# Eight TensorE fillers, squares on ScalarE and weights' low halves on VectorE, in a new order of the first seven units

## Chip, cores and metric

One NeuronCore of one Trainium2 chip. The metric is the device time of one execution, in microseconds (us). TensorE's matmuls, VectorE (DVE), ScalarE (ACT), GpSimd (POOL) and SyncE (SP, which issues the DMAs) run side by side and meet at semaphores.

## What is computed

`x` is 16 x 256 x 256, float32. A layer normalisation, attention with 16 heads of 128 over 4 key/value heads, and a quantised linear layer follow, both added to their input:

```python
x = x + attention(layernorm(x), wq, wk, wv, wo)   # causal, first 4 keys and a window of 32
x = x + ffn(layernorm(x), weight, bias)           # int8-rounded x and weight, 256 -> 256
# attention: q = x wq.T, k = x wk.T, v = x wv.T; softmax(q k.T / sqrt(128), masked) v; then wo.T
```

## The kernel before

Work is cut into 64 **units**: unit u is batch `b = u // 4` and key/value group `g = u % 4`, with its four query heads. Every matmul of the attention runs in float16 with each operand split into a high half (rounded) and a low half (what rounding left), and three products for the pairs high-high, high-low, low-high (`PAIRS`).

The steps of a unit are functions on each engine's queue. On TensorE: `q_fill(u, f)` (L436, half f of the queries, 12 matmuls), `scores(u)` (L466, 27), `p_transpose(u)` (L510, 9), `pv(u, j)` (L539, L540) and `out_proj(u)` (L557, 24); per batch `x_transpose` (L392), `k_fill` (L404) and `v_fill` (L415). What they leave in PSUM is taken out in two steps: ScalarE makes the high half (`q_high` L829, `k_high` L816, `v_high` L824, `o_high` L875), then VectorE subtracts it from PSUM for the low half (`q_low` L1044, `k_low` L1034, `v_low` L1039, `o_low` L1071). The softmax goes VectorE `s_mask` (L1052), `s_peak` (L1057), GpSimd `s_shift` (L1439), ScalarE `exps` (L836), VectorE `probs` (L1062 to L1066), GpSimd `p_norm` (L1450), ScalarE `p_high` (L865), GpSimd `p_low` (L1456), TensorE `p_transpose`, ScalarE `pt_evac` (L845). The normalisation is `ln_stats` (L1018), `ln_rstd` on GpSimd, `ln_norm` (L1028, writes `xn`), `ln_split` on ScalarE and `ln_low` (L1408) on GpSimd.

**Weights.** Before its first use each weight tile (k, v, q0 to q3, o0 to o3; 128 x 1024 numbers each) gets one power of two as its scale. ScalarE sums the squares (`weight_squares`, L799, an activation with an accumulator, read out by a second instruction); TensorE adds that over the partitions and spreads it (`scale_sums`, L367); VectorE makes the scale (`scale`, L1162 to L1167); ScalarE writes the high half (`weight_high`, L805) and VectorE the low half (`weight_low`, L1182: one `scalar_tensor_tensor` with the weight and its high half as inputs, both in SBUF). Four things are different. The output weights' squares are made by GpSimd (`squares`, L1418) and summed by TensorE over columns (`column_sums`, L379, 8 matmuls of one column each a tile), a `column_copy` (L1186) on VectorE putting the sum where `scale_sums("o")` reads it. The low halves of v, o2 and o3 are made by GpSimd in two instructions each (`weight_scaled` L1427, `weight_low` L1433). The scale of k stands first, and the first thing on TensorE is 13 products of `small_ones` with itself (L641) whose result nobody reads.

**Order.** Every engine runs its queue in order. For the units up to the scores of unit 6 the order of calls is written out by hand for each engine; from t = 7 on a loop `for t in range(FIRST, NU - 3)` gives each engine the same turn: scores(t), pv(t-2), both halves of q_fill(t+1), one k or v fill of the next batch, p_transpose(t-1), out_proj(t-2) and what VectorE, ScalarE and GpSimd owe to them. An order for the last three units follows, again by hand. Before the loop TensorE does out_proj(4) last; `scores(7)` opens the loop. A second line of waits: `scores(u)` needs both q_low(u), and from unit 2 on also pt_evac(u-2), whose PSUM bank it takes; `q_fill(u, f)` needs q_low(u-1, f); `pv(u, j)` needs o_low(u-1, j).

SyncE issues the loads in one queue: x of batch 0, wk, wq part 0, idh (the identity for transposes), wv, x of batch 1, wq part 1, the mask, wq parts 2 and 3, wo parts 0 to 3, and so on.

## Time and profile before

| | |
|---|---|
| median of 3 runs | 616.41 us (615.7 to 616.91) |
| the profiled execution's own time | 616.56 us |
| its span, first to last instruction | 614.8 us |
| mean granted TensorE clock | 0.988 of 2.4 GHz |
| TensorE busy | 593.4 us, 97% |
| VectorE busy | 544.4 us, 89% |
| ScalarE busy | 394.6 us, 64% |
| GpSimd busy | 337.3 us, 55% |

Busy time is the time in which an instruction of the engine was under way, so an instruction that is held by something outside it counts as busy. In the rows further down a line is an instruction or a group of equal ones: its start, its length, its engine, the line of the code, what it writes and reads, and in square brackets how long its engine was idle before and whose result it waited for. Consecutive instructions of an engine overlap a little, so that lengths add up to somewhat more than the time that passes. A window's line gives the same by stretch.

### The profile page before, as it was taken

The numbers are of one execution on the slowest core, as the hardware profiler recorded it, in microseconds if no ns is written. First come the engines' busy times: TensorE is split into PE (matmuls) and PEld (weight loads), VectorE is DVE, ScalarE is ACT, GpSimd is POOL, SyncE is SP. The second block draws the span as 40 slices with busy tenths as digits, with TensorE's granted clock in tenths as the row PEclk, the third lists the DMA queues.
The fourth block names the chain that finished last, engine by engine and source line by source line (L and its number), as shares of the span: only waits on it lengthen the run. The fifth ranks groups of instructions, "written<-read, shape, count | busy, mean of one in ns | idle before, by whom it ended". The sixth has DMA issues, their size and how long they took to land.

```text
span 614.8 us, 18062 instructions
## 1 busy us (share of the span) xinstructions
PE 593.4 (97%) x7566; PEld 523.8 (85%) x7566; DVE 544.4 (89%) x1072; ACT 394.6 (64%) x617; POOL 337.3 (55%) x320
## 2 busy tenths in 40 slices
PE   7699999999999999999999999999999999999994
PEld 6488878898888989889898988989898898989883
DVE  6999999898998989899898989979898897989886
ACT  6588646656656766665676666667666666765660
POOL 2667753564745556474555647455564645646563
PEclk8899999999999999999999999999999999999997
DMA  8565205060421506042160604316060421505001
GB/s 294 188 139 139 65 24 122 18 156 19 92 67 56 118 18 156 19 99 59 40 135 20 155 18 91 67 39 135 19 138 3 103 54 37 120 19 138 2 19 35
DMA packets 36272, 49.69 MB, mean 81 GB/s; under 512 B 2784, under 2 KB 22240, under 8 KB 36192
## 3 DMA queue, kind: packets, MB, share of 16 engines
q1 hardware_dynamic: 36048, 48.41, 31.9%
q8 instruction: 60, 0.98, 0.7%
q14 instruction: 20, 0.16, 0.1%
q10 hardware_dynamic: 144, 0.13, 0.1%
HBM read 35.42 MB, written 12.58 MB: 78 GB/s over the span
## 4 chain that ended last, share of the span: by engine, by line
PE 83%; DVE 11%; issue 2%; ACT 2%; POOL 2%; POOLq 0%; DVEq 0%; ACTq 0%
PE ps L436 24%; PE ps L557 23%; PE ps L466 8%; PE ps L404 6%; PE ps L415 6%; PE ps L510 4%; PE ps L540 4%; PE ps L539 4%; DVE Qs L1044 1%; DVE xn L1028 1%; PE ps L392 1%; PE ps L641 1%; PE ps L603 1%; DVE WqT L1182 1%; DVE sm L1062 1%
## 5 line engine op out<-in xcount | busy, mean ns | idle before, releaser
L436 PE MATMUL ps<-xT,WqT 128*128 128x256 f16 x1536 | 179.4, 273 | 2.2 <-DVE WqT L1182 1.4
L557 PE MATMUL ps<-WoT,pool 128*128 128x256 f16 x1440 | 167.3, 273 | 1.0 <-DVE pool L1071 1.0
L436 PEld LDWEIGHTS ps<-xT,WqT 128*128 128x128 f16 x1536 | 146.8, 98 | 19.0 <-DVE WqT L1182 1.8
L557 PEld LDWEIGHTS ps<-WoT,pool 128*128 128x128 f16 x1440 | 138.1, 98 | 16.3 <-DVE pool L1071 1.3
L1450 POOL TENSOR_TENSOR small<-E,rr 128x576 f32<-128x576 f32 x64 | 73.9, 1154 | 92.3 <-DVE rr L1066 92.3
L875 ACT ACTIVATE pool<-ps 128x512 f16<-128x512 f32 x128 | 69.9, 594 | 83.9 <-PE ps L540 83.8
L829 ACT ACTIVATE Qs<-ps 128x576 f16<-128x576 f32 x128 | 82.7, 646 | 44.4 <-PE ps L436 44.3
L1456 POOL TENSOR_TENSOR PP<-small,PP 128x576 f16<-128x576 f32 x64 | 82.2, 1284 | 50.3 <-ACT PP L865 50.3
L1439 POOL TENSOR_TENSOR Sm<-Sm,mx 128x576 f32<-128x576 f32 x64 | 74.9, 1170 | 46.2 <-DVE mx L1057 45.0
L1044 DVE TENSOR_TENSOR Qs<-ps,Qs 128x576 f16<-128x576 f32 x128 | 92.9, 727 | 4.5 <-ACT Qs L829 4.5
L1071 DVE SCALAR_TENSOR_TENSOR pool<-ps,pool 128x512 f16<-128x512 f32 x128 | 82.1, 680 | 0.0
L1052 DVE TENSOR_TENSOR Sm<-ps,mask 128x576 f32<-128x576 f32 x64 | 47.6, 744 | 27.7 <-PE ps L466 27.7
L845 ACT ACTIVATE PT<-ps 128x1024 f16<-128x1024 f16 x64 | 66.0, 1031 | 8.6 <-PE ps L510 8.6
L836 ACT ACTIVATE E<-Sm,esc 128x576 f32<-128x576 f32 x64 | 49.6, 774 | 25.8 <-POOL Sm L1439 25.8
L466 PE MATMUL ps<-Kw,Qs 128*128 128x64 f16 x1728 | 61.5, 194 | 4.2 <-DVE Qs L1044 4.0
L466 PEld LDWEIGHTS ps<-Kw,Qs 128*128 128x128 f16 x1728 | 59.1, 98 | 7.6 <-DVE Qs L1044 5.3
L1062 DVE TENSOR_REDUCE sm<-E 128x9 f32<-128x576 f32 x64 | 48.0, 750 | 15.2 <-ACT E L836 15.2
L1057 DVE TENSOR_REDUCE mx<-Sm 128x9 f32<-128x576 f32 x64 | 48.2, 753 | 2.0
L404 PE MATMUL ps<-xT,WkT 128*128 128x256 f16 x384 | 48.4, 277 | 0.3 <-DVE Vn L1039 0.3
L415 PE MATMUL ps<-WvT,xT 128*128 128x512 f16 x192 | 47.4, 383 | 0.4 <-POOL WvT L1433 0.4
L865 ACT ACTIVATE PP<-small 128x576 f16<-128x576 f32 x64 | 43.8, 685 | 2.3 <-POOL small L1450 2.1
L510 PE MATMUL ps<-idh,PP 128*128 128x128 f16 x576 | 42.6, 219 | 0.5 <-POOL PP L1456 0.5
(129 smaller groups left out, 913.7 us busy)
## 6 DMA issues: line engine op xcount, KB each, us to landing
values<-Vn SPq DMA_DIRECT2D x32, 256.0 KB, 2.0
VW<-values SPq DMA_DIRECT2D x16, 480.0 KB
big<-values SPq DMA_DIRECT2D x16, 480.0 KB
X<-in_L_attn_x SPq DMA_DIRECT2D x16, 256.0 KB, 8.4
...
```

Source lines behind the costliest of these rows:

```text
L404: a = pe.matmul(banks[k_bank(b, f)][:, j * 256:j * 256 + 256], WkT[:, k, wl, g * 128:g * 128 + 128], xT[:, b % 2, k, xl, :], start=(n == 1 ...
L415: a = pe.matmul(banks[v_bank(b, t)][:, :], xT[:, b % 2, k, xl, t * 128:t * 128 + 128], WvT[:, k, wl, :], start=(n == 1), stop=(n == 6))
L436: a = pe.matmul(banks[BANK_Q[f]][:, j * 256:j * 256 + 256], WqT[:, k, wl, h * 128:h * 128 + 128], xT[:, b % 2, k, xl, :], start=(n == 1), ...
L466: a = pe.matmul(banks[BANK_S[c]][:, (s - s0) * KEYS:(s - s0 + 1) * KEYS], Qs[:, p, ql, s * 128:s * 128 + 128], Kw[:, b % 2, g, kl, w, :], ...
L557: a = pe.matmul(out_view(b, t), OT[:, p, ol, h, t * 128:t * 128 + 128], WoT[:, 4 * g + h, wl, :], start=first, stop=(end and g == KV - 1), ...
L829: act.activation(dst[0], src, ACT.Copy).then_inc(q_h, 1)
L875: act.activation(OT[:, u % 2, 0, :, cols], src, ACT.Copy, scale=1.0 / P_UP).then_inc(o_h, 1)
L1044: dve.tensor_tensor(dst[1], src, dst[0], ALU.subtract).then_inc(q_l, 1)
L1071: dve.scalar_tensor_tensor(OT[:, u % 2, 1, :, cols], src, 1.0 / P_UP, OT[:, u % 2, 0, :, cols], ALU.mult, ALU.subtract).then_inc(o_l, 1)
L1439: pool.tensor_tensor(Sm[:, p], Sm[:, p], mx[:, p, :].unsqueeze(2).to_broadcast([128, NT, KEYS]), ALU.subtract).then_inc(s_d, 1)
L1450: pool.tensor_tensor(Pn[:, p], E[:, p], rr[:, p, :].unsqueeze(2).to_broadcast([128, NT, KEYS]), ALU.mult).then_inc(p_n, 1)
L1456: pool.tensor_tensor(PP[:, p, :, 1, :], Pn[:, p], PP[:, p, :, 0, :], ALU.subtract).then_inc(p_l, 1)
```

## The change

The four squares of the output weights become `weight_squares` on ScalarE, each with a column of `am` of its own (it grows to 10 columns), and `scale_sums("o")` adds the four columns in PSUM; `column_sums`, `column_copy` and the constant `one` go. The low halves of v, o2 and o3 become `weight_low` on VectorE, and GpSimd does nothing on weights any more (with them go `squares`, `weight_scaled` and GpSimd's `weight_low`). Eight more products of `small_ones` follow the sum of k. idh is loaded ahead of wq part 0. `scale_sums("v")` moves ahead of k_fill(0, 0). Otherwise all calls up to the loop stay, in another order on each of the four queues. The loop and the end are the same. The diff without its first declarations, the constant and the removed GpSimd functions:

```diff

     load_x(0)
     sp.dma_start(w_tile("k"), wk_v).then_inc(ld_k, 16)
+    sp.dma_start(idh[:, :], idh_d).then_inc(ld_idh, 16)
     sp.dma_start(w_tile("q0"), wq_v[0]).then_inc(ld_q[0], 16)
-    sp.dma_start(idh[:, :], idh_d).then_inc(ld_idh, 16)
     sp.dma_start(w_tile("v"), wv_v).then_inc(ld_v, 16)
     load_x(1)
     sp.dma_start(w_tile("q1"), wq_v[1]).then_inc(ld_q[1], 16)
...

         if name == "k":
             pe.wait_ge(cst_ok, 3)
-        elif name != "o":
+        else:

             pe.wait_ge(w_s[SUMS_ORDER[SUMS_ORDER.index(name) - 1]], 1)
-        pe.wait_ge(w_am[name], 1)
-        c = SCALES[name]
-        pe.matmul(all_sums(name), small_ones[:, :], am[:, c:c + 1], start=True, stop=True).then_inc(w_all[name], 1)
-
-    def column_sums(name):
-
-        if name == "o0":
+        if name == "o":

             pe.wait_ge(v_l, 2)
-            pe.wait_ge(cst_ok, 5)
-        pe.wait_ge(w_sq[name], 1)
-        sq = w_squares(name)
-        for h in range(4):
-            for k in range(2):
-                a = pe.matmul(banks[BANK_OUT][:, 0:1], sq[:, h, 128 * k:128 * k + 128], one[:, 0:1],
-                              start=(name == "o0" and h == k == 0), stop=(name == "o3" and h == 3 and k == 1))
-        a.then_inc(w_col, 1)
+        n = KV if name == "o" else 1
+        pe.wait_ge(w_am[name], n)
+        for c in range(SCALES[name], SCALES[name] + n):
+            a = pe.matmul(all_sums(name), small_ones[:, :], am[:, c:c + 1], start=(c == SCALES[name]), stop=(c == SCALES[name] + n - 1))
+        a.then_inc(w_all[name], 1)

     def x_transpose(b):

...
     for _ in range(13):
         pe.matmul(banks[BANK_S[0]][:, 0:128], small_ones[:, :], small_ones[:, :], start=True, stop=True)
     scale_sums("k")
+    for _ in range(8):
+        pe.matmul(banks[BANK_S[0]][:, 0:128], small_ones[:, :], small_ones[:, :], start=True, stop=True)
     pe.wait_ge(ld_idh, 16)
     x_transpose(0)
     scale_sums("q0")
+    scale_sums("v")
     pe.wait_ge(xt_ok, 1)
     k_fill(0, 0)
-    scale_sums("v")
     scale_sums("q1")
     q_fill(0, 0)
     q_fill(0, 1)
+    v_fill(0, 0)
+    v_fill(0, 1)
+    scores(0)
     scale_sums("q2")
-    v_fill(0, 0)
-    scores(0)
-    v_fill(0, 1)
     q_fill(1, 0)
     q_fill(1, 1)
     scale_sums("q3")

     pe.wait_ge(v_l, 1)
     k_fill(0, 1)
-    column_sums("o0")
     scores(1)
-    column_sums("o1")
-    column_sums("o2")
     q_fill(2, 0)
+    q_fill(2, 1)
+    q_fill(3, 0)
     x_transpose(1)
-    q_fill(2, 1)
+    scale_sums("o")
+    q_fill(3, 1)
+    p_transpose(0)

     pe.wait_ge(xt_ok, 2)
     pe.wait_ge(k_l, 2)
     k_fill(1, 0)
-    column_sums("o3")
-    q_fill(3, 0)
-    p_transpose(0)
-    scale_sums("o")
-    q_fill(3, 1)
     scores(2)
+    q_fill(4, 0)
+    pv(0, 0)
+    pv(0, 1)

     pe.wait_ge(k_l, 3)
     v_fill(1, 0)
-    pv(0, 0)
-    pv(0, 1)
-    q_fill(4, 0)

     pe.wait_ge(s_m, 3)
     v_fill(1, 1)
+    q_fill(4, 1)
+    p_transpose(1)

     pe.wait_ge(v_l, 3)
     k_fill(1, 1)
-    p_transpose(1)
-    q_fill(4, 1)
     scores(3)
     q_fill(5, 0)
-    x_transpose(2)
     pv(1, 0)
     pv(1, 1)
+    x_transpose(2)
+    q_fill(5, 1)
     p_transpose(2)
-    q_fill(5, 1)
+    out_proj(0)
     scores(4)
-    out_proj(0)
-    q_fill(6, 0)
+
+    pe.wait_ge(xt_ok, 3)
+    pe.wait_ge(k_l, 4)
+    k_fill(2, 0)
     pv(2, 0)
     pv(2, 1)
+    q_fill(6, 0)
     p_transpose(3)
     q_fill(6, 1)
     scores(5)
-
-    pe.wait_ge(xt_ok, 3)
-    pe.wait_ge(k_l, 4)
-    k_fill(2, 0)
     out_proj(1)
-    q_fill(7, 0)
-    p_transpose(4)
-    pe.wait_ge(k_l, 5)
-    v_fill(2, 0)
-    scores(6)
     pv(3, 0)
     pv(3, 1)
     out_proj(2)
+    p_transpose(4)
+    q_fill(7, 0)
+    scores(6)
     pv(4, 0)
     pv(4, 1)
+    pe.wait_ge(k_l, 5)
+    v_fill(2, 0)
     out_proj(3)
     q_fill(7, 1)
     pe.wait_ge(v_l, 5)
...

         act.wait_ge(w_loaded(name), 16)
         src, hi, _, _ = w_views(name, None)
-        act.activation(hi, src, ACT.Square, accum_out=am[:, SCALES[name]:SCALES[name] + 1]).then_inc(w_am[name], 1)
+
+        n, c = ("o", SCALES["o"] + int(name[1])) if name[0] == "o" else (name, SCALES[name])
+        act.activation(hi, src, ACT.Square, accum_out=am[:, c:c + 1]).then_inc(w_am[n], 1)

     def weight_high(name, js=(0, 1)):
         whole = len(js) == 2
...
     weight_squares("q1")
     weight_high("v")
     k_high(0, 0)
+    q_high(0, 0)
+    weight_high("q1")
+    q_high(0, 1)
     weight_squares("q2")
-    q_high(0, 0)
-    q_high(0, 1)
-    weight_high("q1")
-    weight_high("q2")
     v_high(0, 0)
+    weight_squares("o0")
+    v_high(0, 1)
     weight_squares("q3")
     ln_split(1)
-    v_high(0, 1)
     q_high(1, 0)
+    weight_high("q2")
     q_high(1, 1)
+    weight_high("q3")
+    weight_squares("o1")
     exps(0)
-    k_high(0, 1)
-    weight_high("q3")
+    weight_squares("o2")
     q_high(2, 0)
-    x_evac(1)
+    weight_squares("o3")
     q_high(2, 1)
     p_high(0)
-    k_high(1, 0)
+    k_high(0, 1)
     q_high(3, 0)
+    x_evac(1)
+    weight_high("o0")
     pt_evac(0)
     exps(1)
+    k_high(1, 0)
+    q_high(3, 1)
+    q_high(4, 0)
+    weight_high("o1")
+    p_high(1)
+    o_high(0, 0)
+    ln_split(2)
+    v_high(1, 0)
+    v_high(1, 1)
+    o_high(0, 1)
+    exps(2)
+    pt_evac(1)
+    q_high(4, 1)
+    k_high(1, 1)
+    p_high(2)
     weight_high("o2")
-    weight_high("o0")
-    q_high(3, 1)
-    v_high(1, 0)
-    p_high(1)
-    weight_high("o1")
-    ln_split(2)
-    exps(2)
-    v_high(1, 1)
-    q_high(4, 0)
-    pt_evac(1)
-    o_high(0, 0)
-    o_high(0, 1)
-    p_high(2)
-    q_high(4, 1)
+    x_evac(2)
+    exps(3)
+    pt_evac(2)
+    o_high(1, 0)
     q_high(5, 0)
-    x_evac(2)
-    pt_evac(2)
-    exps(3)
-    k_high(1, 1)
-    o_high(1, 0)
+    o_high(1, 1)
     q_high(5, 1)
-    o_high(1, 1)
     p_high(3)
+    o_high(2, 0)
+    o_high(2, 1)
     q_high(6, 0)
-    o_high(2, 0)
     pt_evac(3)
     exps(4)
-    o_high(2, 1)
     k_high(2, 0)
+    weight_high("o3")
+    q_high(6, 1)
     p_high(4)
-    q_high(6, 1)
-    weight_high("o3")
-    pt_evac(4)
-    v_high(2, 0)
     o_high(3, 0)
     o_high(3, 1)
+    pt_evac(4)
+    o_high(4, 0)
     exps(5)
+    v_high(2, 0)
+    o_high(4, 1)
     q_high(7, 0)
-    o_high(4, 0)
-    exps(6)
     ln_split(3)
     p_high(5)
-    o_high(4, 1)
     q_high(7, 1)
     v_high(2, 1)
+    exps(6)
     pt_evac(5)

     for t in range(FIRST, NU - 3):
...
     weight_low("k", (1,))
     x_evac(0)
     scale("q0")
+    ln_stats(1)
     exp_scale(0)
-    ln_stats(1)
     scale("v")
     weight_low("q0", (0,))
     weight_low("q0", (1,))
     scale("q1")
-    ln_norm(1)
-    exp_scale(1)
+    weight_low("v")
     k_low(0, 0)
-    scale("q2")
     q_low(0, 0)
     q_low(0, 1)
     weight_low("q1")
+    v_low(0, 0)
+    ln_norm(1)
+    scale("q2")
     s_mask(0)
-    v_low(0, 0)
+    v_low(0, 1)
     s_peak(0)
+    scale("q3")
+    q_low(1, 0)
+    q_low(1, 1)
     weight_low("q2")
-    q_low(1, 0)
-    v_low(0, 1)
-    q_low(1, 1)
-    scale("q3")
+    weight_low("q3")
     probs(0)
     s_mask(1)
-    k_low(0, 1)
-    weight_low("q3")
     q_low(2, 0)
     s_peak(1)
     q_low(2, 1)
-    column_copy()
     ln_stats(2)
+    scale("o")
+    k_low(0, 1)
+    exp_scale(1)
+    q_low(3, 0)
+    weight_low("o0")
+    probs(1)
     k_low(1, 0)
-    scale("o")
-    q_low(3, 0)
-    probs(1)
+    exp_scale(2)
+    ln_norm(2)
     s_mask(2)
-    exp_scale(2)
+    q_low(3, 1)
     s_peak(2)
-    ln_norm(2)
+    q_low(4, 0)
     v_low(1, 0)
-    weight_low("o0")
-    q_low(3, 1)
+    v_low(1, 1)
+    o_low(0, 0)
     probs(2)
-    v_low(1, 1)
-    q_low(4, 0)
-    o_low(0, 0)
+    o_low(0, 1)
+    q_low(4, 1)
     s_mask(3)
-    o_low(0, 1)
+    exp_scale(3)
     s_peak(3)
-    q_low(4, 1)
-    exp_scale(3)
+    ln_stats(3)
+    k_low(1, 1)
     weight_low("o1")
-    q_low(5, 0)
     probs(3)
     o_low(1, 0)
+    o_low(1, 1)
     s_mask(4)
-    o_low(1, 1)
+    q_low(5, 0)
+    s_peak(4)
     q_low(5, 1)
-    s_peak(4)
-    ln_stats(3)
-    k_low(1, 1)
     o_low(2, 0)
+    o_low(2, 1)
+    ffn_weight_scale()
+    weight_low("o2")
     probs(4)
-    q_low(6, 0)
     s_mask(5)
     k_low(2, 0)
+    s_peak(5)
+    q_low(6, 0)
     q_low(6, 1)
-    ffn_weight_scale()
-    o_low(2, 1)
-    s_peak(5)
+    o_low(3, 0)
+    o_low(3, 1)
+    weight_low("o3")
+    ln_norm(3)
+    ffn_weight_round()
+    probs(5)
     s_mask(6)
     v_low(2, 0)
-    o_low(3, 0)
-    o_low(3, 1)
     s_peak(6)
-    probs(5)
-    ln_norm(3)
-    o_low(4, 0)
-    probs(6)
     out_scale()
     ffn_residual(0)
+    o_low(4, 0)
     o_low(4, 1)
-    ffn_stats(0)
     q_low(7, 0)
     q_low(7, 1)
-    ffn_weight_round()
+    ffn_stats(0)
+    probs(6)
     v_low(2, 1)

     for t in range(FIRST, NU - 3):
...
     ln_rstd(0)
     ln_low(0)
     ln_rstd(1)
-    weight_scaled("v")
-    weight_low("v")
-    squares("o0")
-    squares("o1")
+    ln_low(1)
     s_shift(0)
-    squares("o2")
-    ln_low(1)
     p_norm(0)
-    squares("o3")
+    s_shift(1)
     p_low(0)
-    s_shift(1)
     ln_rstd(2)
     p_norm(1)
+    p_low(1)
     s_shift(2)
-    p_low(1)
     ln_low(2)
     p_norm(2)
     p_low(2)
     s_shift(3)
-    weight_scaled("o2")
     p_norm(3)
+    ln_rstd(3)
     p_low(3)
     s_shift(4)
-    weight_low("o2")
     p_norm(4)
-    ln_rstd(3)
     p_low(4)
-    weight_scaled("o3")
     s_shift(5)
-    weight_low("o3")
+    p_norm(5)
+    p_low(5)
     s_shift(6)
-    p_norm(5)
     ln_low(3)
-    p_low(5)
+    f_rstd(0)
     p_norm(6)
-    f_rstd(0)

     for t in range(FIRST, NU - 3):
         b, g = divmod(t, KV)
```

## Rows read from the trace of the kernel before

**Rows 1.** Stretches: length, busy PE, PEld, DVE, ACT, POOL, granted clock, DMA, GB/s.

```profile
106.74:586.00 479.26, 478.72 (x6248) 426.57 (x6244) 424.75 (x827) 311.28 (x490) 260.65 (x250) 1.00 0.30 71
...
12.15:50.68 38.53, 31.78 (x350) 25.15 (x348) 35.57 (x65) 28.91 (x44) 26.52 (x19) 0.94 0.59 168
...
51.24:87.60 36.36, 35.01 (x450) 30.15 (x448) 35.32 (x66) 24.50 (x38) 27.59 (x23) 1.00 0.35 81
```

**Rows 2.** Timeline, TensorE, scores of units 3 and 7: start, length, line.

```profile
51.24 0.95 PE L466 MATMUL ps<-Kw,Qs 128*128 128x64 f16 x27
...
87.60 0.95 PE L466 MATMUL ps<-Kw,Qs 128*128 128x64 f16 x27
```

**Rows 3.** The chain of waits, units 7 to 9: start, length, piece.

```profile
98.07 0.06 PE ps L539
...
98.98 2.62 PE ps L436 x24
...
106.74 0.79 PE ps L466 x27
...
112.58 0.50 PE ps L510 x9
```

**Rows 4.** Timeline, VectorE and GpSimd side by side: start, length, engine, line.

```profile
5.99 0.73 DVE L1028 TENSOR_SCALAR xn<-X,mv,rs 128x256 f32<-128x256 f32 x2 [1.18 <-POOL rs L1404]
...
13.95 3.03 DVE L1182 SCALAR_TENSOR_TENSOR WqT<-big,up,WqT 128x512 f16<-128x512 f32 x2
...
17.36 3.65 DVE L1028 TENSOR_SCALAR xn<-X,mv,rs 128x256 f32<-128x256 f32 x2
...
18.93 3.84 POOL L1418 TENSOR_TENSOR WoT<-pool 128x1024 bf16<-128x1024 f32 x2
...
24.02 1.27 DVE L1182 SCALAR_TENSOR_TENSOR WqT<-big,up,WqT 128x1024 f16<-128x1024 f32 x1
...
35.13 2.44 DVE L1182 SCALAR_TENSOR_TENSOR WqT<-big,up,WqT 128x1024 f16<-128x1024 f32 x1
...
69.99 1.89 POOL L1427 TENSOR_TENSOR pool<-pool,up 128x1024 f32<-128x1024 f32 x1 [0.35 <-ACT WoT L805]
...
70.31 1.60 DVE L1197 TENSOR_SCALAR ft<-ft 128x2 f32<-128x2 f32 x1
```

**Rows 5.** Timeline, TensorE at the start, and one stretch with its granted clock.

```profile
1.11 5.74 PE L641 MATMUL ps<-small_ones 128*128 128x128 f32 x26 [1.11 <-DVE small_ones L1229]
...
8.89 0.62 PE L392 MATMUL ps<-idh,xhl 128*128 128x128 f16 x8 [1.92 <-DMA idh<-in_idh]
...
10.52 2.72 PE L404 MATMUL ps<-xT,WkT 128*128 128x256 f16 x12
...
11.00:12.00 1.00, 1.00 (x7) 0.69 (x6) 0.93 (x6) 1.00 (x4) 0.00 (x0) 0.50 1.05 399
```

**Rows 6.** Timeline, VectorE: the scale of q0 and the peak of unit 2.

```profile
10.69 0.16 DVE L1162 TENSOR_SCALAR dn<-ps 128x1 int32<-128x1 int32 x1 [0.26 <-PE ps L367]
...
44.75 0.75 DVE L1057 TENSOR_REDUCE mx<-Sm 128x9 f32<-128x576 f32 x1
```

**Rows 7.** The profile page, part 5: groups of instructions, busy, mean ns, idle before.

```profile
L1439 POOL TENSOR_TENSOR Sm<-Sm,mx 128x576 f32<-128x576 f32 x64 | 74.9, 1170 | 46.2 <-DVE mx L1057 45.0
...
L836 ACT ACTIVATE E<-Sm,esc 128x576 f32<-128x576 f32 x64 | 49.6, 774 | 25.8 <-POOL Sm L1439 25.8
...
L845 ACT ACTIVATE PT<-ps 128x1024 f16<-128x1024 f16 x64 | 66.0, 1031 | 8.6 <-PE ps L510 8.6
```

**Rows 8.** Timeline, one sum of squares on ScalarE with its read-out.

```profile
16.14 1.05 ACT L799 ACTIVATE WqT<-big 128x1024 f16<-128x1024 f32 x1
...
17.09 0.20 ACT L799 ACTIVATION_READ_ACCUMULATOR WqT<-big 128x1 f32 x1
```

**Rows 9.** Waits of ScalarE, 12.15 to 50.7 us: total, times, longest.

```profile
ACT Qs L829 <- PE ps L436: 3.9, 6, 1.0
...
ACT WqT L805 <- DVE up L1167: 2.6, 1, 2.6
```

More of the change, by code:

```diff
@@ L80, in build @@
         diag = sb("diag", [128, 2, 128], F32)
-        am = sb("am", [128, 7], F32)
-        one = sb("one", [128, 2], BF16)
+        am = sb("am", [128, 10], F32)
         up = sb("up", [128, 7], F32)
@@ L176, in build @@
         w_am = {n: sem(f"w_am_{n}") for n in SCALES}
-        w_sq = {n: sem(f"w_sq_{n}") for n in TILES[6:]}
-        w_col = sem("w_col")
         w_all = {n: sem(f"w_all_{n}") for n in SCALES}
@@ L182, in build @@
         w_l = {n: sem(f"w_l_{n}") for n in TILES}
-        w_c = {n: sem(f"w_c_{n}") for n in ("v", "o2", "o3")}
         def w_tile(name):
@@ L205, in w_views @@
             return (w_tile(name)[:, :, n0:n1], wt[:, :, 0, at + n0:at + n1], wt[:, :, 1, at + n0:at + n1], SCALES[name])
-        def w_scaled(name):
-            if name[0] == "o":
-                return w_tile(name)
-            return E[:, :, :, :].rearrange("p u s k -> p (u s k)")[:, 0:1024].rearrange("p (k r) -> p k r", k=2)
         def all_sums(name):
             return banks[BANK_OUT if name == "o" else BANK_O[1]][:, SCALES[name]:SCALES[name] + 1]
-        def w_squares(name):
-            h0 = 4 * int(name[1])
-            return WoT[:, h0:h0 + 4, 1, :].bitcast(BF16)
         x_v = x_d.rearrange("b (t p) d -> b p t d", p=128)
@@ L1230, in _ @@
             dve.memset(ones[:, :], 1.0).then_inc(cst_ok, 1)
-            dve.memset(one[:, :], 1.0).then_inc(cst_ok, 1)
             dve.memset(VW[0][64:128, :, 1, :].bitcast(F32), 0.0).then_inc(z_ok, 1)
@@ L1414, in f_rstd @@
                 pool.tensor_tensor(rs2[:, :, 0], rs2[:, :, 1], cst[:, 2:4], ALU.pow).then_inc(f_rs, 1)
-            def squares(name):
-                pool.wait_ge(w_loaded(name), 16)
-                pool.tensor_tensor(w_squares(name), w_tile(name), w_tile(name), ALU.mult).then_inc(w_sq[name], 1)
-            def weight_scaled(name):
-                src, _, _, c = w_views(name, None)
-                if name == "v":
-                    pool.wait_ge(w_s[name], SCALE_OPS)
-                else:
-                    pool.wait_ge(w_h[name], 2)
-                pool.tensor_tensor(w_scaled(name), src, up[:, c:c + 1].unsqueeze(2).to_broadcast(list(src.shape)), ALU.mult).then_inc(w_c[name], 2)
-            def weight_low(name):
-                _, hi, lo, _ = w_views(name, None)
-                pool.wait_ge(w_h[name], 2)
-                pool.wait_ge(w_c[name], 2)
-                pool.tensor_tensor(lo, w_scaled(name), hi, ALU.subtract).then_inc(w_l[name], 2)
             def s_shift(u):
```

3 lines of the change are left out of this document (removed).

## Prediction

> **What bounds the kernel now.** I read the end first, then walked back. From the second turn of the loop to shortly before the end TensorE is busy for 478.7 of 479.3 us [rows 1]: the loop is bound by TensorE and nothing in it is edited. So the kernel's time is the start of the loop plus a constant. The loop's first instruction is the scores of unit 7, at 87.60 us [rows 2]; the span is 614.8 us and the profiled execution's own time 616.56, so 528.96 us follow that start. The whole question is what happens to 87.60.
>
> I cut the 87.60 us at the scores of unit 3, at 51.24 [rows 2]: stretch A before it, stretch B of 36.36 us behind it. In B the chain of waits gives TensorE's issue cost of each piece [rows 3]: 2.62 us for 24 matmuls of q_fill, hence 1.31 for a half of 12, and the same 1.31 for a k_fill or v_fill and 2.62 for an out_proj, which feed as many columns; 0.79 for a scores; 0.91 for a pv (98.07 to 98.98); 0.50 for a p_transpose of nine, so 0.45 for an x_transpose of eight. B holds 6 q halves, 3 k/v fills, 4 p_transposes, 1 x_transpose, 4 scores, 4 pv and 5 out_proj: 7.9 + 3.9 + 2.0 + 0.45 + 3.2 + 3.6 + 13.1 = 34.1 us. The new order holds the same pieces between the same two points. TensorE's floor for B is 34.1, and the kernel loses only 2.2 us to it. In A it is different: from 12.15 to 50.68 VectorE is busy 35.57 of 38.53 us, TensorE 31.78, ScalarE 28.91, GpSimd 26.52 [rows 1]. VectorE sets the pace, and part of its busy time is no work but waiting inside an instruction, as follows.
>
> **What leaves VectorE's path.** Two xn instructions took 3.65 us from 17.36, and 0.73 at 5.99. The second time GpSimd was at the low half of v and then at squares (3.84 from 18.93). The low half of q3 took 2.44 against 1.27 for q1's of the same size; the two halves of q0's took 3.03 for the same elements [rows 4]. I count 2.9 + 1.2 + 1.5 (3.03 less 1.27 and a second instruction's start, about 0.25) = 5.6 us of stalls in A that lie beside GpSimd's work on weights. That work goes: four squares and the three pairs for v, o2, o3. In B the same shows once, at 70.31: 1.60 us for a two-element instruction under a GpSimd instruction of 1.89 from 69.99 [rows 4], about 1.4 lost.
>
> **What comes onto VectorE.** The low halves of v, o2 and o3, at 1.27 each if undisturbed, v in A and the others in B. The upper bound of one is 2.44 [rows 4]. I take 1.27, because with the weights gone GpSimd runs only softmax steps, and each of these (shift, product, low half of P) is released by VectorE's own reduction or reciprocal just before. The column copy and a memset go, at nothing: one is an element per partition, the other lies in the idle start.
> What the rows show is that VectorE is held only while GpSimd is inside an instruction. The Trainium skill (SBUF — State Buffer, Who interferes with whom) says that a VectorE instruction with two SBUF inputs contends with a GpSimd instruction that reads SBUF, and that whichever issued first holds the other for the whole instruction. A weight's low half has two SBUF inputs, so this speaks against moving three more of them to VectorE; it is the second rival below.
>
> **The first products.** 26 records took 5.74 us [rows 5], 0.22 each, so eight more products are 16 records or 3.5 us, from 6.9 to 10.3. They are no longer covered: x_transpose(0), at 8.89 today [rows 5], starts at 10.3, ends at 10.9, and with its copy on VectorE the scale of q0 starts at 11.6 instead of 10.69 [rows 6]: 0.9 us later. That idh is loaded ahead of q0 on SyncE's queue takes away the wait for it and gains nothing behind these products; q0 is needed by ScalarE later than it lands, so I price its delay at nothing (0.5 at worst). In return the clock: k_fill(0,0) took 2.72 us, twice the 1.31 of an equal fill later, with a granted clock of 0.50, which is 1.2 GHz, after TensorE had stood idle from 6.9 to 8.9 [rows 5]. If the busy engine keeps 2.4 GHz, that fill is 1.3 shorter. It ends ahead of VectorE's and ScalarE's queues either way, so I book zero (0 to 1.0 gained).
>
> **Stretch A, summed.** VectorE ran from the scale of q0 (10.69) to the end of unit 2's peak (44.75 + 0.75 = 45.5) [rows 6]: 34.8 us. Less 5.6 of stalls, plus what now stands ahead of that peak: v's low 1.27, o0's low 1.27, q_low(3,1) 0.65 (an estimate: it passes as many elements as the peak, which took 0.75 with the overlap of its neighbours) and ln_norm(2) 0.73, together 3.9. That gives 33.1 us from 11.6: 44.7. Behind it stand GpSimd's shift 1.17, ScalarE's exponential 0.77 and the copy of PT(1) 1.03 [rows 7], and scores(3) could start at 47.7. Other steps of VectorE (ln_stats, k_low) only swap places within the sum.
> ScalarE has a floor of its own. It worked 28.91 us from 12.15 to 50.68 [rows 1]; its part to the same copy gains four squares at 1.05 + 0.20, counted without overlap [rows 8], 5.0 in all. The high half of o2 leaves and a high half of q0 comes in, which cancels. So 33.9 us from about 12.15: 46.0 if it never waits. It waited 9.6 us before; 2.6 for a scale stuck on VectorE behind the xn stall, 3.9 for q fills [rows 9]. The squares fill such gaps only where they stand in the right place of an in-order queue: a square waiting for its load would hold the evacuations behind it, but GpSimd's squares of o0 and o1 ran from 18.93 back to back [rows 4], so those loads have landed by then, and only the length counts. Squares of o0 now stand ahead of v_high(0,1), those of o1 ahead of the first exponentials. For waits of ScalarE that fall on the path I add 1.0 (0 to 5): scores(3) at 48.8, **2.4 us earlier**.
>
> **Stretch B.** 2.2 us were lost on TensorE's floor. VectorE is full here too, 35.32 of 36.36 [rows 1]; it gets two lows (2.5) and loses 1.4 of stall, and ffn_weight_round now stands ahead of the last q_low of unit 7 rather than behind. Against it, o0's low, q_low(3,1) and one normalisation are done earlier, and v_fill(2,0) is drawn between, so that TensorE has other work while P of unit 4 is made. I take 1.2 lost instead of 2.2 (0 to 3.5): **1.0 us earlier**. The loop's first turns, which start in the wake of B, may give back a little: I take 0.2, a guess between 0 and 0.5.
>
> The scale of o now sums four columns in eight records instead of two. That is 0.5 to 1 us of TensorE in A, which has it to spare, and the 32 column sums go. The four squares need no column sum to be copied, which shortens that path.
>
> **The sum.** 2.4 + 1.0 + 0.2 = 3.6 us off the profiled 616.56: **612.9 us**. The median of the runs is 616.41, 0.15 less, which I ignore.
>
> **Rivals.**
> - *TensorE's floor is met.* ScalarE adds no wait: scores(3) at 47.7, B at 34.1, loop at 81.8: 5.8 earlier, 610.8 us. For it: the stalls of A are the largest loss seen. Against: three engines would have to mesh without a gap. Chance 0.14 for this and anything below 611.
> - *The stalls move with the lows.* If the lows of v and o0 in A and one of o1 to o3 in B each start just behind a GpSimd instruction, each costs the 1.17 that q3's cost (2.44 less 1.27). A keeps 0.1 of its gain, B loses its: 616.3 us, no measurable change. This is what the rule of the skill named above would make of the time. Against: GpSimd loses four squares of 1.9 us each and six instructions on weights of about the same length [rows 4]. Chance 0.14.
> - *ScalarE becomes the bound, slower.* Its queue from the high halves of q0 to the copy of PT(1) has a floor of 46.0. Of the 9.6 us that it waited only the 2.6 behind the stalled scale [rows 9] are surely gone. If the other 7.0 stay, since q evacuations still wait for fills while squares push everything behind them, the copy ends at 53.0 and scores(3) starts 1.8 later than now; B keeps its loss: 618.4 us. It decides from 5.2 us of ScalarE idle in A. For it: today's waits on fills. Against: those fills waited for VectorE. Chance 0.12.
> - The forecast has 0.60, on its own from 611 to 615.2.
>
> **How the numbers follow.** 0.2% of this time is 1.2 us, about what a measurement of this kernel can tell from no change. Below 615.2 lie the forecast, the floor case and a small part of the second rival: 0.76. Within 615.2 to 617.6: 0.13. Above: 0.11. The range takes in most of the floor case and of the second rival: 610.3 to 617.0, leaving out some 6% below and 11% above.
>
> **What would show it.** Right: scores(3) near 48.8 and scores(7) near 84; the xn instructions of batch 1 at 0.7 together; each weight low near 1.3; no idle TensorE of 3 us before scores(0); granted clock 1.00 at 11 to 12 us; ScalarE nearly without idle from 12 to 45. Wrong: scores(3) at 51 or later with ScalarE waiting (third rival), or lows over 2 us (second). If the time from scores(7) to the end is not 527.2 us of the span within 0.5, my view that the loop is a constant fails.

## The result

The changed kernel takes 608.36 us (median of 4 runs, 607.61 to 608.53); the kernel before, beside it, 616.66 (4 runs). The ratio is 0.9863 with a 95% interval of 0.9851 to 0.9875: 8.3 us faster. The forecast was 612.9 with a range from 610.3 to 617.0: right in sign, less than half of the size, and the time lies outside the range.

The page of the changed kernel, part 1 and the TensorE clock of part 2:

```profile
PE 592.2 (98%) x7556; PEld 523.7 (86%) x7556; DVE 536.1 (88%) x1073; ACT 397.3 (66%) x625; POOL 313.7 (52%) x310
PEclk8999999999999999999999999999999999999997
```

VectorE (DVE) is busy 8.3 us less than before (544.4), although three low halves of 1.28 us have come onto it. So about 12 us have gone in which one of its instructions was held, as far as busy time tells. Instruction by instruction, against the same one in the changed kernel, the timelines give as much: 5.7 us in A and 4.6 in B, which the next sections show, and 2.1 in three more (xn at 45.41, the low half of o0 at 47.50, `diag` at 87.22). GpSimd (POOL) is busy 23.6 us less.

The scores of units 3 and 7 in the changed kernel, which answer to [rows 2], and the stretches that they cut, which answer to [rows 1] (length, busy PE, PEld, DVE, ACT, POOL, granted clock, DMA share, GB/s):

```profile
45.47 0.95 PE L442 MATMUL ps<-Kw,Qs 128*128 128x64 f16 x27
79.72 0.95 PE L442 MATMUL ps<-Kw,Qs 128*128 128x64 f16 x27
```

```profile
10.44:45.47 35.03, 32.45 (x336) 25.69 (x336) 33.05 (x75) 33.55 (x56) 12.21 (x13) 0.95 0.71 206
45.47:79.72 34.25, 34.25 (x449) 30.25 (x450) 32.79 (x70) 24.00 (x37) 16.98 (x17) 1.00 0.38 80
```

| us | before | forecast | after |
|---|---|---|---|
| A: scores(3) starts | 51.24 | 48.8 | 45.47 |
| B: scores(3) to scores(7) | 36.36 | 35.4 | 34.25 |
| C: scores(7) to the end of the span | 527.2 | 527.0 | 526.8 |

Stretch B has met TensorE's floor of 34.1. The loop is the constant it was taken for. Of the 8.2 us between the two profiled executions' own times (616.56 and 608.33), 7.9 lie in A and B (5.8 and 2.1), where the forecast looked for them; it asked for too little in both.

The chain of waits of the changed kernel shows from where on TensorE alone sets the pace (start, length, piece):

```profile
29.86 0.68 DVE Qs L1024
30.54 0.05 issue
30.58 1.49 PE ps L412 x12
32.07 0.45 PE ps L368 x8
32.52 0.84 PE ps L356 x8
33.36 1.33 PE ps L412 x12
34.69 0.50 PE ps L486 x9
```

From q_fill(3, 0) at 30.58 nearly every piece is PE. In the kernel before this state was reached for good only inside the loop, at the scores of unit 8 (97.12). The 0.84 for L356 are the eight records of `scale_sums("o")`, which are on the path now; the forecast had given them to a TensorE with time to spare.

### The profile page after: what moved, and what is told of

Read it like the earlier page. It is cut to its first block, busy times and chain, and to the rows that moved or that the text cites. A ratio compares the mean times of both kernels' runs of the same rounds, so it can differ in the third digit from the quotient of the medians.

```text
span 606.5 us, 18038 instructions
## 1 busy us (share of the span) xinstructions
PE 592.2 (98%) x7556; PEld 523.7 (86%) x7556; DVE 536.1 (88%) x1073; ACT 397.3 (66%) x625; POOL 313.7 (52%) x310
## 4 chain that ended last, share of the span: by engine, by line
PE 90%; DVE 4%; ACT 2%; issue 1%; POOL 1%; DMA 0%; POOLq 0%; DVEq 0%
PE ps L412 26%; PE ps L533 25%; PE ps L442 8%; PE ps L380 7%; PE ps L391 6%; PE ps L486 5%; PE ps L516 5%; PE ps L515 5%; PE ps L368 1%; PE ps L579 1%; PE ps L548 1%; PE ps L564 1%; ACT Qs L805 1%; DMA X<-in_L_attn_x 0%; DVE Qs L1024 0%
## 5 line engine op out<-in xcount | busy, mean ns | idle before, releaser
L1408 POOL TENSOR_TENSOR small<-E,rr 128x576 f32<-128x576 f32 x64 | 73.7, 1152 | 109.6 <-DVE rr L1046 109.5
```

The source lines that it names most:

```text
L1408: pool.tensor_tensor(Pn[:, p], E[:, p], rr[:, p, :].unsqueeze(2).to_broadcast([128, NT, KEYS]), ALU.mult).then_inc(p_n, 1)
```

## The experiments

Three theories were set against each other: **stalls** (VectorE's instructions on SBUF are held while GpSimd is inside one), **order** (the new sequence takes waits away by itself), **clock** (the products keep TensorE at 2.4 GHz). A fourth, that ScalarE sets the pace, was the forecast's slower rival. Each kernel ran beside the kernel before on the same chip; all ratios are against that one. In the diffs the kernel's own helper names stand for their steps.

| run | median us | ratio, interval | scores(3) | scores(7) |
|---|---|---|---|---|
| moves in the old order (e4) | 612.63 | 0.9938 [0.9923, 0.9953] | 47.39 | 84.49 |
| order alone, old work on GpSimd (e8) | 613.12 | 0.9950 [0.9934, 0.9967] | 48.33 | 84.18 |
| products and idh alone (e5) | 616.11 | 0.9991 [0.9981, 1.0000] | 50.35 | 86.70 |
| changed, without the products (e1) | 609.49 | 0.9882 [0.9867, 0.9897] | 45.53 | 79.78 |
| lows alone (e2) | 616.59 | 0.9999 [0.9988, 1.0010] | 51.34 | 88.70 |
| squares alone (e3) | 614.65 | 0.9981 [0.9971, 0.9992] | 51.36 | 87.45 |
| changed, 16 products (e10) | 608.76 | 0.9876 [0.9861, 0.9891] | 45.92 | 80.16 |
| changed, seven more in gaps (e12) | 607.77 | 0.9861 [0.9846, 0.9876] | 44.76 | 79.00 |
| changed, squares on GpSimd (e7) | 611.86 | 0.9927 [0.9912, 0.9942] | 49.19 | 83.44 |
| changed, no squares of wo (e14) | 608.05 | 0.9865 [0.9848, 0.9881] | 44.60 | 78.85 |
| changed, two splits on GpSimd (e11) | 608.04 | 0.9870 [0.9850, 0.9890] | 44.72 | 78.97 |
| e11 and e12 together (e13) | 607.83 | 0.9860 [0.9845, 0.9875] | 44.60 | 78.85 |
| changed, rounding one place later (e15) | 609.58 | 0.9892 [0.9879, 0.9906] | 44.80 | 80.69 |
| changed, again (e16) | 608.94 | 0.9878 [0.9858, 0.9898] | 47.22 | 81.46 |
| e12 again (e17) | 608.01 | 0.9865 [0.9850, 0.9880] | 44.66 | 78.91 |

The last two columns are from the one profiled execution, in us from the span's start. For e2, e3 and e16 that execution was slower than the run's median, by 1.0, 1.7 and 1.2 us, and for e1 it was 1.1 faster. In e8, e5 and e10 to e15 and in e17 its TensorE clock never fell after the start; in the changed kernel, e1, e2, e3, e4, e7 and e16 it did, which by the last section of experiments is worth up to 2.6 us. Differences of under 1 us between two rows of these columns are therefore not read as effects of an edit.

### The moves without the order, the order without the moves

e4 is the kernel before with only these edits, GpSimd's steps on the same weights, the column sums and the column copy taken away, and the eight products and idh first, as in the change:

```diff
 # VectorE
     scale("q1")
+    weight_low("v")
...
+    weight_low("o2")
     o_low(2, 0)
...
+    weight_low("o3")
     v_low(2, 0)
 # ScalarE
     v_high(0, 0)
+    weight_squares("o0")
...
+    weight_squares("o1")
     exps(0)
...
+    weight_squares("o2")
     q_high(2, 0)
+    weight_squares("o3")
```

> The kernel before in its old order, with all the moves of the change: low halves of v, o2, o3 on VectorE, squares of the output weights on ScalarE, eight more products, idh loaded first. Theory 'stalls' (the gain of 8.3 us is that VectorE is no longer held inside instructions by GpSimd's work on weights, 5.6 us in stretch A and 1.4 in B): most of the gain is here, 5 us or more, 611.5 us or less; scores(3) near 47. Rival 'order' (the old order has waits that only the new one takes away): 2 us or less gained, 614.5 us or more.

e8 is the changed kernel with these steps put back on GpSimd and taken from VectorE and ScalarE, and with `column_sums` and `column_copy` back ahead of `scale("o")`:

```diff
 # GpSimd
     ln_rstd(1)
+    weight_scaled("v")
+    weight_low("v")
+    squares("o0")
+    squares("o1")
     ln_low(1)
     s_shift(0)
+    squares("o2")
     p_norm(0)
+    squares("o3")
...
     s_shift(4)
+    weight_scaled("o2")
+    weight_low("o2")
...
     s_shift(5)
+    weight_scaled("o3")
+    weight_low("o3")
```

> The changed kernel's order on all engines with the eight products, but GpSimd does its old work again: squares of o0 to o3 and the low halves of v, o2 and o3 in two instructions each, and TensorE its column sums. Theory 'stalls': VectorE is held again, as before the change, and the gain is mostly gone: 613 to 617 us, with xn of batch 1 or q0's low halves long again. Rival 'order': gain of 5 us or more stays, 611.5 or less.

Measured: 612.63 and 613.12, gains of 3.9 and 3.4 us. e4 lies between the two theories; e8 lies just inside what 'stalls' gave for it, but with a gain of 3.4 that 'stalls' does not explain. Each part is worth about half. Both runs have the eight products and idh first, which bring 0.4 alone (e5), so the two parts add up to 6.9, and about 1.4 of the 8.3 come only with both. Where they act differs. In A the moves bring 3.85 us in the old order (51.24 to 47.39), of which the products and idh have 0.9 (e5: 50.35); the order brings another 1.9 on top. In B the moves alone cost 0.7 (37.10 against 36.36), since they put two lows of 1.3 on a full VectorE; the order alone brings 0.5; together they bring 2.1. So in B there is a clear gain only with both.

In A the forecast's stalls are all there to see. VectorE in e4, where GpSimd does no weights, is short at q0's halves, v and xn; in e8, with them, it is not (start, length, engine, line, what):

```profile
12.79 1.41 DVE L1191 SCALAR_TENSOR_TENSOR WqT<-big,up,WqT 128x512 f16<-128x512 f32 x2
...
16.16 0.73 DVE L1037 TENSOR_SCALAR xn<-X,mv,rs 128x256 f32<-128x256 f32 x2
...
30.69 1.28 DVE L1191 SCALAR_TENSOR_TENSOR WqT<-big,up,WqT 128x1024 f16<-128x1024 f32 x1
```

```profile
12.50 3.03 DVE L1186 SCALAR_TENSOR_TENSOR WqT<-big,up,WqT 128x512 f16<-128x512 f32 x2
...
18.48 1.98 DVE L1186 SCALAR_TENSOR_TENSOR WqT<-big,up,WqT 128x1024 f16<-128x1024 f32 x1
...
20.98 1.70 DVE L1032 TENSOR_SCALAR xn<-X,mv,rs 128x256 f32<-128x256 f32 x2
...
26.75 3.67 DVE L1186 SCALAR_TENSOR_TENSOR WqT<-big,up,WqT 128x1024 f16<-128x1024 f32 x2
```

The three instructions of [rows 4] that took 3.03, 3.65 and 2.44 take 1.41, 0.73 and 1.28 in e4: 5.7 us less, the 5.6 of the forecast. One low of v (1.28) is added, and 3.85 arrive, with the products and idh in them.

Why B needs both is in the same two timelines. In B of e4 GpSimd does nothing on weights, and still six instructions of VectorE are held, 3.2 us together, all beside steps of the softmax or the normalisation; two of them are the first fence. In B of e8 the new order has freed these, and four are held, 5.3 us together, each beside a step on o2's or o3's low half (L1431 and L1437); two of them, with that step, are the second fence. Without a hold the same instructions take 0.73, 0.15, 0.16 and 0.47. In the changed kernel neither kind is left.

```profile
75.67 1.53 DVE L1037 TENSOR_SCALAR xn<-X,mv,rs 128x256 f32<-128x256 f32 x2
...
79.29 1.05 DVE L1181 TENSOR_TENSOR osc<-dn 128x1 f32<-128x1 f32 x1
```

```profile
62.54 2.13 POOL L1437 TENSOR_TENSOR WoT<-pool,WoT 128x1024 f16<-128x1024 f32 x1 [0.17 <-POOL pool L1431]
62.63 2.06 DVE L1206 SCALAR_TENSOR_TENSOR ft<-ft 128x2 f32<-128x2 f32 x1
...
72.83 2.29 POOL L1437 TENSOR_TENSOR WoT<-pool,WoT 128x1024 f16<-128x1024 f32 x1 [0.17 <-POOL pool L1431]
73.05 2.34 DVE L1219 TENSOR_SCALAR diag<-idf,ft 128x128 f32<-128x128 f32 x2
```

### Each move alone

e2 is the kernel before with only the low halves of e4, e3 with only its squares (and without the column sums and the copy):

```diff
 # e2, VectorE
     scale("q1")
+    weight_low("v")
...
+    weight_low("o2")
     o_low(2, 0)
...
+    weight_low("o3")
     v_low(2, 0)
```

```diff
 # e3, ScalarE
     v_high(0, 0)
+    weight_squares("o0")
...
+    weight_squares("o1")
     exps(0)
...
+    weight_squares("o2")
     q_high(2, 0)
+    weight_squares("o3")
```

> The kernel before, only the low halves of v, o2 and o3 moved to VectorE; squares stay on GpSimd. Theory 'stalls': of the three stalls in stretch A the one of q0's low halves (1.5 us) goes, the squares start earlier and still hold xn or the low half of v, 1.3 us of work is added: 615 to 617 us. Rival 'work' (it is the pairs on GpSimd that made v_fill(0,0) and the scores of unit 0 late, not the stalls): 614 or less.

> The kernel before, only the squares of the output weights moved to ScalarE. Theory 'stalls': the part of xn's stall behind 18.9 us and q3's 1.2 go, 2.5 us gained at most: 614 to 615. Rival 'ScalarE bound': four squares of 1.1 push its queue, nothing gained or slower, 616.5 or more. With the run before this tells whether the moves are worth more together (3.9 us) than apart, since xn waits for whichever GpSimd instruction is under way.

Measured: 616.59, nothing, and 614.65, 1.9 us. Both as the stalls would have it, and less together than in one: 1.9 + 0.0 against e4's 3.9 (of which e5 below has 0.4). xn waits for the GpSimd instruction that is under way. Without v's pair the squares simply start earlier, at 16.12, and hold it longer than before (VectorE and GpSimd in e2):

```profile
16.12 4.49 POOL L1421 TENSOR_TENSOR WoT<-pool 128x1024 bf16<-128x1024 f32 x2 [2.89 <-DMA pool<-in_L_attn_wo]
...
16.88 3.88 DVE L1028 TENSOR_SCALAR xn<-X,mv,rs 128x256 f32<-128x256 f32 x2
```

### Squares back on GpSimd, and no squares at all

e7 is the changed kernel with only the four squares back on GpSimd, each where e8 has it. e14 is the changed kernel without the four squares, whose sums are set to a constant instead:

```diff
 # e7, GpSimd
     ln_rstd(1)
+    squares("o0")
+    squares("o1")
     ln_low(1)
     s_shift(0)
+    squares("o2")
     p_norm(0)
+    squares("o3")
```

```diff
 # e14, ScalarE
-    weight_squares("o0")
...
-    weight_squares("o1")
...
-    weight_squares("o2")
...
-    weight_squares("o3")
 # VectorE
+    dve.memset(am[:, 6:10], 1.0).then_inc(w_am["o"], 4)
```

> The changed kernel, in its new order, with only the squares of the output weights back on GpSimd and the column sums back on TensorE. Theory 'stalls': VectorE's instructions with two SBUF inputs (q1's low half at 18.9 us, q2's and q3's at 25.7) stand next to squares of 1.9 us and are held: 609.5 to 611. Rival 'ScalarE bound' (in the new order ScalarE is busy 33.6 of 35.0 us of stretch A, so four squares less there give time back): 608 or less.

> The changed kernel with the four sums of squares of the output weights left out altogether (their sums are a constant, so this part of the scale's calculation is not done). Theory 'ScalarE sets the pace of stretch A now': scores(3) 2 to 4.5 us earlier, 604 to 606.5. Theory 'VectorE does': the four squares lie in ScalarE's slack, within 1 of 608.4.

Squares on GpSimd: 611.86, 3.5 us slower than the change and 0.9 above what was expected of 'stalls'. Stalls are the larger part: in e7's timeline q1's low takes 2.62 where it took 1.28 in the changed kernel, and q2's and q3's together 3.67 where they took 2.47. That is 2.5 of the 3.7 us by which scores(3) is later; on the chain of waits the column sums and their copy add about 0.6 between q_fill(3, 0) and q_fill(3, 1), and the rest was not traced.

```profile
16.72 3.75 POOL L1425 TENSOR_TENSOR WoT<-pool 128x1024 bf16<-128x1024 f32 x2 [3.71 <-DMA pool<-in_L_attn_wo]
...
18.93 2.62 DVE L1186 SCALAR_TENSOR_TENSOR WqT<-big,up,WqT 128x1024 f16<-128x1024 f32 x1
...
26.86 3.67 DVE L1186 SCALAR_TENSOR_TENSOR WqT<-big,up,WqT 128x1024 f16<-128x1024 f32 x2
```

No squares at all: 608.05, and scores(7) at 78.85, no earlier than in e12 and e11 (79.00, 78.97), which keep them. The theory that ScalarE sets the pace falls, although it is the busiest engine of A (33.55 of 35.03 us). Five us of its work are free in an execution whose clock does not fall, where the chain of waits runs over VectorE up to q_fill(3, 0) (e12, e14). In the changed kernel's own profile, with its slow q fills, that chain runs over ScalarE from 16.0 to 25.0; what the squares cost in such an execution was not measured; when they go it waits for q fills instead (e14's waits of ScalarE from 12 to 45 us: total, times, longest):

```profile
ACT Qs L805 <- PE ps L412: 3.4, 3, 2.3
```

The squares fill time in which ScalarE would wait for TensorE. Moving the high halves of x to GpSimd gave nothing that the clock (below) does not explain:

```diff
 # e11, ScalarE
-    ln_split(1)
...
-    ln_split(2)
 # GpSimd
+    ln_split(1)
     ln_low(1)
...
+    ln_split(2)
     ln_low(2)
```

> The changed kernel with the high halves of the normalised x of batches 1 and 2 made by GpSimd instead of ScalarE. If ScalarE sets the pace: up to 1.1 us earlier, 607.3. If GpSimd's two more instructions hold VectorE or the shift of unit 0 behind them: 608.4 or more.

> As the run before and the seven products in TensorE's gaps, which gave 0.6 us alone. If both are independent, 606.7 to 607.3; if ScalarE's queue is not what sets the pace, 607.8 or more.

Measured: 608.04, and 607.83 together with e12's products (e13), neither apart from its neighbours; the first lies between its two expectations, the second at the lower end of the range for a ScalarE that does not set the pace.

### One block moved one place

```diff
 # e15, on the changed kernel, VectorE
-    ffn_weight_round()
     probs(5)
+    ffn_weight_round()
     s_mask(6)
```

> The changed kernel with ffn_weight_round (five instructions on SBUF, 1.4 us) one place later on VectorE, behind probs(5), the step that releases GpSimd's product of unit 5. Theory 'place' (the new order gains in stretch B because VectorE's instructions on SBUF stand where GpSimd is idle): one of the five is held, about 1.1 us instead of 0.2, though the work is the same; by TensorE's slack of about 1 us there the time grows by 0 to 1.5. Rival (the stalls come from what GpSimd does on weights alone): every one of the five as short as now.

Measured: 609.58. B grew from 34.25 to 35.89 (44.80 to 80.69). The clock of e15's profiled execution never fell, so it is to be compared with e11 and e17, which start scores(7) at 78.97 and 78.91: 1.7 us later. At the median it is 1.2 us above the change's first measurement and 0.6 above its second (e16). The same two instructions on the timeline, first in the changed kernel and then in e15, where they stand next to GpSimd's product of unit 5 (L1408), a step of the softmax:

```profile
69.14 0.47 DVE L1191 TENSOR_SCALAR diag<-idf,ft 128x128 f32<-128x128 f32 x2
```

```profile
71.57 1.40 DVE L1191 TENSOR_SCALAR diag<-idf,ft 128x128 f32<-128x128 f32 x2
71.73 1.15 POOL L1408 TENSOR_TENSOR small<-E,rr 128x576 f32<-128x576 f32 x1 [5.58 <-DVE rr L1046]
...
78.06 2.79 PE L533 MATMUL ps<-WoT,pool 128*128 128x256 f16 x24 [0.81 <-DVE pool L1051]
```

0.93 us are lost inside one pair of instructions. The rest of the 1.6 that B grew by is, as I read it, that the block now stands behind probs(5) instead of in VectorE's wait for the exponentials; no run separates the two. out_proj(4) then waits for VectorE, 0.81 (third line). The theory 'place' has it: a softmax step of GpSimd holds too, not only its work on weights, and part of what the order does in B is to keep VectorE's SBUF instructions away from such steps. In B of the kernel before, seven instructions were held, and I had priced one. One, the two-element instruction at 70.31, is in [rows 4]; four of the others, from VectorE's timeline of the kernel before:

```profile
55.41 1.61 DVE L1182 SCALAR_TENSOR_TENSOR WoT<-pool,up,WoT 128x1024 f16<-128x1024 f32 x1
...
77.95 0.66 DVE L1064 TENSOR_SCALAR sg<-sm 128x9 f32<-128x9 f32 x1
...
78.78 1.53 DVE L1028 TENSOR_SCALAR xn<-X,mv,rs 128x256 f32<-128x256 f32 x2
...
82.40 1.05 DVE L1172 TENSOR_TENSOR osc<-dn 128x1 f32<-128x1 f32 x1
```

Against 1.28, 0.17, 0.73 and 0.15 for the same instructions in the changed kernel that is 0.3 + 0.5 + 0.8 + 0.9; two more of sg lost 0.7 and the two-element instruction 1.4: 4.6 us. Of these 1.7 lie beside a step on o2's or o3's low half (the two-element instruction and one of sg, at 58.38), the other 2.9 beside a softmax step or `ln_low`. In the changed kernel none of the seven is held.

### The products and the clock

e5 is the kernel before with only the change's eight products and idh ahead of q0. The others are the changed kernel: e1 without the eight, e10 with sixteen, e12 with seven more in the gaps behind them; e16 is the changed kernel and e17 is e12, both once more.

```diff
 # e1
-            for _ in range(8):
-                pe.matmul(banks[BANK_S[0]][:, 0:128], small_ones[:, :], small_ones[:, :], start=True, stop=True)
```

```diff
 # e10
-            for _ in range(8):
+            for _ in range(16):
```

```diff
 # e12
     x_transpose(0)
+    for _ in range(2):
+        pe.matmul(banks[BANK_S[0]][:, 0:128], small_ones[:, :], small_ones[:, :], start=True, stop=True)
     scale_sums("q0")
+    for _ in range(2):
+        pe.matmul(banks[BANK_S[0]][:, 0:128], small_ones[:, :], small_ones[:, :], start=True, stop=True)
     scale_sums("v")
...
     k_fill(0, 0)
+    for _ in range(3):
+        pe.matmul(banks[BANK_S[0]][:, 0:128], small_ones[:, :], small_ones[:, :], start=True, stop=True)
     scale_sums("q1")
```

> The changed kernel without its eight products after the sum of k; idh stays first. Theory 'stalls': x_transpose(0) starts when ln_low ends, at 8.7, with or without them, and ScalarE and VectorE set the pace behind it: within 0.7 of 608.4. Rival 'clock': TensorE at 1.2 GHz from about 10 to 13.5, k_fill(0,0) and q_fill(0,0) late by 1 to 2 us, 609.5 or more.

> The kernel before with only the eight more products and idh loaded ahead of q0. Theory 'stalls': nothing to be gained where VectorE is held by GpSimd, 616.7 within 0.7. Rival 'clock' (the fuller TensorE keeps 2.4 GHz at the start, and this is worth what the falls to 1.2 GHz cost, about 1.3 us for k_fill(0,0)): 615.4 or less.

> The changed kernel with 16 more products behind the sum of k instead of 8. At 0.127 us a record, as these eight took, they end at 10.7, so x_transpose(0) starts 1.8 later. Theory 'start' (a delay of q0's scale goes through to the end in full, so the 1.4 us by which the eight products ended earlier than forecast are 1.4 us of the missed gain): 609.4 to 610.3. Rival (slack behind it takes the delay): within 0.5 of 608.4.

> The changed kernel with seven products more in the gaps of TensorE between x_transpose(0) and q_fill(0,0) (2, 2 and 3). The granted clock was 0.50 from 11.85 to 15.1. If the gaps caused that fall and the slow fills cost time, 607.3 or less; if ScalarE's and VectorE's queues set the pace, within 0.6 of 608.4.

> The changed kernel itself, beside the next run on the same chip. 608.4; its granted clock at 12 us is 1.00 in some executions and 0.50 in others, 0.7 us apart.

> The changed kernel with the seven products in TensorE's gaps, again. Theory 'clock': every execution keeps 2.4 GHz to 16 us, 607.7, 0.4 to 0.8 below the run beside it. Rival (chance): no difference.

Measured: 609.49 without products (1.1 us above the change's median), 616.11 with them alone, 608.76 with sixteen, 607.77 and 608.01 with seven more in the gaps, against 608.94 for the change on the same chip as the last. The expectations fare unevenly: e5 has the number of 'stalls', e1 just misses that of 'clock', e10 falls in its rival's range, e12 misses both of its ranges narrowly, and e17 beats its neighbour by 0.9, slightly more than forecast. e1's interval (0.9867 to 0.9897) overlaps those of both measurements of the change (0.9851 to 0.9875, 0.9858 to 0.9898), so what the eight products are worth by themselves is not settled. What lies behind these times is for how long TensorE falls to 1.2 GHz in each *execution*. The clock from 12 to 13 us in the profiled executions of e12, of the changed kernel and of e1 (length, busy PE, granted clock, DMA share, GB/s for the first; all engines for the others):

```profile
12.00:13.00 1.00, 1.00 (x12) 1.00 1.07 390
```

```profile
12.00:13.00 1.00, 1.00 (x7) 0.67 (x6) 0.93 (x6) 1.00 (x2) 0.81 (x2) 0.50 1.06 388
```

```profile
12.00:13.00 1.00, 1.00 (x6) 0.74 (x5) 0.93 (x6) 1.00 (x2) 0.70 (x2) 0.50 1.04 382
```

In the changed kernel's profiled execution the clock stood at 1.2 GHz from about 11.7 to 15.1 and scores(7) came at 79.7; in its second profile (e16) it stood there from about 12.4 to 19.3, the two halves of q_fill(0) took 5.28 us instead of 2.78, and scores(7) came at 81.5. In the profiled executions of e12, e17, e11, e13 and e14 it never fell, and scores(7) came at 78.9 to 79.0. TensorE's first gaps lie just behind the products, and which of the three happens changes from one execution to the next: the nine runs of the changed kernel (four and e16's five) go from 607.5 to 611.0; the mean clock of the two slowest is 0.990, that of the three fastest 0.995 or 0.996. The eight runs of e12 and e17 go from 607.5 to 608.6, with 0.994 to 0.996 in all, and so do e13's four. Of the thirteen runs of the changed kernel and e11, which have no products in the gaps, eight have a mean clock of 0.993 or less. So the products in the gaps keep the clock up and leave the best executions as they were: 0.6 and 0.9 us at the median, while the intervals overlap.

Sixteen products end at 10.5; the scale of q0 comes 1.1 later than in e11, whose clock did not fall either, and scores(7) 1.2 later (80.16 against 78.97). By this pair of profiled executions a delay there goes through in full, as the theory 'start' said. Its time, 608.76, is the rival's all the same: against the changed kernel, which pays for its clock, only 0.4 of the delay shows.

e1's profiled execution, its fastest, starts scores(7) as early as the changed kernel's (79.78), with its clock at 0.50 from about 8.1 to 15.0. The scale of q0 comes at 10.53 there, against 10.44.

**A version that is at least as good:** the changed kernel with the seven products in the gaps (e12, e17), 607.77 and 608.01 us. Against the kernel before it is 1.4% faster. Against the change itself its runs lie closer together; a gain of the median is not shown, since the intervals overlap.

## Why the forecast was wrong

**Right:** what bounds the kernel, the cut at the scores of units 3 and 7, TensorE's floor of 34.1 for B (measured 34.25, with no gap), the constant loop (526.8 against 527.2; 0.4 came back where 0.2 was forecast), and the 5.6 us of stalls in A next to GpSimd's weights (5.7 in e4). The low halves that moved took 1.28 each, the 1.27 taken. The rivals in which stalls move with the lows or ScalarE binds did not come. The floor rival did, and more: its 81.8 for scores(7) became 79.7. Two sums are off by 0.1 us, with no weight: 47.7 and 1.0 make 48.7, not 48.8, and 616.56 less 3.6 is 613.0. One reason given for lows of 1.27 was wrong and did no harm: GpSimd's low half of P is released by ScalarE (`PP`, with idle time of 0.79 before it), not by VectorE.

**Wrong, in the terms of the sum:** A was forecast 2.4 shorter and is 5.8 shorter. The missing 3.4 us are three terms of the forecast's sum. They say where the sum was off, not what each would have brought alone: from 30.58 on the chain of waits is TensorE's own work (busy 14.80 of the 14.89 us to scores(3)), and the copy of PT(1), which the sum aimed at, ends at 45.32, 0.15 before it.

- *The start of the chain*, +0.9 forecast. The eight products were priced at the pace of the first 26 records, 0.22 us, and took 0.127. VectorE came to the scale of q0 at 10.44, not at 11.6. The price was that of a TensorE that had not reached full pace; [rows 5] had the hint, x_transpose(0) at 8.89 in 0.62, as fast as the next one in the changed kernel (0.61 at 31.91). In the changed kernel:

```profile
6.63 2.03 PE L620 MATMUL ps<-small_ones 128*128 128x128 f32 x16
...
8.85 0.61 PE L368 MATMUL ps<-idh,xhl 128*128 128x128 f16 x8 [0.19 <-POOL xhl L1385]
```

  This is 1.15 us. e10 against e11 shows that such a delay does go through in full, so the step's logic held and its size failed.
- *VectorE from that scale to the peak of unit 2*, 33.1 forecast, 31.7 measured. I had left all waits of the old order in the sum, because nothing told me which would go. 1.4 us, and 2.1 where the clock does not fall (31.0 in e12). e4 against the change puts 1.9 us of A on the order; which waits these are was not taken apart.
- *ScalarE's waits on the path*, 1.0 taken. Behind the peak 3.3 us passed, forecast 4.1. e14 shows that the squares on ScalarE's full queue cost next to nothing. 0.8 us. A full engine is not yet the bound: the sum of its queue (46.0 for the copy of PT(1)) was compared with another sum and not with who waits for whom. The squares lay in its waits for q fills [rows 9], as the forecast's text allowed and its sum did not.

B was forecast 1.0 shorter and is 2.1 shorter. The step that failed is the list of stalls: I looked for long VectorE instructions beside GpSimd's weight work only and found 1.4 us, where the same timeline holds 4.6. Nearly all of the rest sits beside softmax and normalisation steps, and there the new order acts: e4 keeps these holds, e8 does not have them, and e15 makes one anew. The changed kernel adds 2.5 us of lows to B and still has VectorE busy 2.5 less (32.79 against 35.32 in [rows 1]).

The Trainium skill (SBUF — State Buffer, Who interferes with whom) says that a VectorE instruction in a two-port mode contends with GpSimd, that one with two SBUF inputs contends with a GpSimd instruction that reads SBUF, and that whichever issued first blocks the other for the whole instruction. The traces agree: `osc`, with two SBUF inputs of one element a partition, took 1.05 us instead of 0.15 beside `p_low`, and the two-element instruction at 70.31 ended at 71.91, as GpSimd's at 69.99 did at 71.88. I had weighed it against the change, because three more such instructions come onto VectorE. Applied to all of VectorE's instructions in the old order it would have spoken for it.

The clock was booked at zero with up to 1.0. By execution it costs 0 to 2.6 us (78.9, 79.7 or 81.5 for scores(7) of the same code or nearly). The sign that the forecast named, a granted clock of 1.00 at 11 to 12 us, came only in part: it fell at 11.7. What the eight products gain at the median is not settled (e1, e5).
